# Keys of a chunk in parts of 512 and 384 instead of 448 and 448, and a new order of the first blocks' loads and query products

## The reference, cut to what matters

```python
q = (query @ Wq + bq).reshape(B, L, NKV, G, HDIM)          # 64 x 4096, 8 groups of 4 heads
k_, v_ = jnp.split(kv @ Wkv + bkv, 2, axis=-1)             # 6272 x 1024 each
scores = jnp.einsum('blkgd,bmkd->bkglm', q, k) * scale
attn = jax.nn.softmax(scores, axis=-1)
o = jnp.einsum('bkglm,bmkd->blkgd', attn, v).reshape(B, L, NHEAD * HDIM)
return o @ Wo + bo
```

## Time and profile before

| what | value |
|---|---|
| median of 3 runs | 1019.71 us |
| lowest and highest | 1017.62 and 3386.0 us |
| the profiled execution's own time | 1017.49 us |
| its span, first to last instruction | 1015.7 us |
| mean granted TensorE clock | 0.998 |
| PE busy | 996.8 us (98%) |
| DVE busy | 744.5 us (73%) |
| ACT busy | 587.4 us (58%) |
| POOL busy | 441.6 us (43%) |

### The profile page before, as it was taken

How to read it: one execution, slowest core, us unless ns; L and a number is a source line. 1 busy time by engine, 2 the same in 40 slices (tenths; PEclk the granted TensorE clock), 3 DMA queues, 4 the chain that set the end, 5 groups by cost and what they waited for, 6 DMA issues and landing times.

```text
span 1015.7 us, 20355 instructions
## 1 busy us (share of the span) xinstructions
PE 996.8 (98%) x7083; PEld 922.3 (91%) x7083; DVE 744.5 (73%) x1680; ACT 587.4 (58%) x1254; POOL 441.6 (43%) x641
## 2 busy tenths in 40 slices
PE   8989999999999999999999999999999999999998
PEld 6769999999999999999999999999999999999744
DVE  5677877676877777777877778677777768776666
ACT  5455666565656656566665656565665655565431
POOL 2243544444434545344454445434444444333231
PEclk9999999999999999999999999999999999999999
DMA  9763332333424333333333333333333237464895
GB/s 323 229 218 128 107 129 98 133 120 131 138 93 134 106 129 112 113 131 130 129 107 115 107 133 122 125 118 117 128 107 133 93 125 245 161 220 157 254 329 162
DMA packets 90085, 149.59 MB, mean 147 GB/s; under 512 B 10528, under 2 KB 44976, under 8 KB 89984
## 3 DMA queue, kind: packets, MB, share of 16 engines
q1 hardware_dynamic: 88224, 146.42, 43.6%
q10 hardware_dynamic: 1424, 1.51, 0.4%
q0 software_dynamic: 336, 0.35, 0.1%
HBM read 82.97 MB, written 14.81 MB: 96 GB/s over the span
## 4 chain that ended last, share of the span: by engine, by line
PE 91%; DVE 4%; DMA 2%; ACT 1%; issue 1%; SPq 1%; POOL 0%; DVEq 0%; POOLq 0%; ACTq 0%
PE p_kv L88 16%; PE p_kv L90 16%; PE p_kv L89 15%; PE p_s L88 7%; PE p_s L90 6%; PE p_s L89 6%; PE p_t L769 6%; PE p_o L88 4%; PE p_o L90 4%; PE p_o L89 4%; PE p_s L849 1%; PE p_ot L753 1%; DMA wkv_raw<-in_wkv 1%; DMA ctx_st<-in_ctx_t 1%; PE p_o L783 1%
## 5 line engine op out<-in xcount | busy, mean ns | idle before, releaser
L610 POOL TENSOR_SCALAR slots<-code 128x512 f32<-128x512 bf16 x232 | 147.8, 637 | 247.3 <-DVE slots L1466 164.2
L1210 ACT ACTIVATE pt_hi<-p_t 128x512 fp32r<-128x512 f32 x224 | 110.0, 543 | 117.0 <-PE p_t L769 111.4
L1466 DVE TENSOR_TENSOR slots<-slots 128x512 f32<-128x512 f32 x232 | 169.8, 732 | 1.6 <-POOL slots L610 1.5
L1239 ACT ACTIVATE slots<-code,drop_and_offsets 128x512 f32<-128x512 bf16 x232 | 158.6, 713 | 6.5 <-POOL code L606 3.4
L1198 ACT ACTIVATE v_hi<-p_kv 128x256 fp32r<-128x256 f32 x196 | 75.3, 384 | 139.1 <-PE p_kv L90 138.3
L630 POOL TENSOR_TENSOR slots<-slots 128x512 f32<-128x512 f32 x58 | 77.7, 1339 | 165.5 <-DVE slots L1466 165.5
L1430 DVE TENSOR_TENSOR pt_lo<-p_t,pt_hi 128x512 fp32r<-128x512 f32 x224 | 128.7, 614 | 11.0 <-ACT pt_hi L1210 10.0
L1415 DVE TENSOR_TENSOR v_lo<-p_kv,v_hi 128x256 fp32r<-128x256 f32 x196 | 83.1, 424 | 67.4 <-ACT v_hi L1198 64.7
L88 PE MATMUL p_kv<-wkv_hi,ctx_even_hi 128*128 128x256 f32 x448 | 128.9, 288 | 0.2 <-DVE v_lo L1415 0.2
L89 PE MATMUL p_kv<-wkv_lo,ctx_even_hi 128*128 128x256 f32 x448 | 125.9, 281 | 0.0
L90 PE MATMUL p_kv<-wkv_hi,ctx_even_lo 128*128 128x256 f32 x448 | 125.9, 281 | 0.0
(11 more groups left out here) (261 smaller groups left out, 2717.5 us busy)
## 6 DMA issues: line engine op xcount, KB each, us to landing
probs_r<-probs SPq DMA_DIRECT2D x110, 448.0 KB, 3.7
code<-in_codes SPq DMA_DIRECT2D x58, 256.0 KB, 3.8
scale<-in_scales SPq DMA_DIRECT2D x114, 128.0 KB, 3.1
expanded_weights<-slots SPq DMA_DIRECT2D x56, 256.0 KB, 2.1
ctx_st<-in_ctx_t SPq DMA_DIRECT2D x96, 112.0 KB, 3.0
ring_hi<-expanded_weights SPq DMA_DIRECT2D x22, 256.0 KB, 5.4
ring_lo<-expanded_weights SPq DMA_DIRECT2D x22, 256.0 KB, 5.6
wq_hi<-in_wq SPq DMA_DIRECT2D x4, 1024.0 KB, 7.2
```

The costliest lines, as they stand in the source:

```text
L610: nc.gpsimd.tensor_scalar(slots[:, slot, :], code16[:], LINES[j][0], LINES[j][1], ALU.mult, ALU.add).then_inc(pool_lines, 1)
L1210: nc.scalar.activation(pt_hi[:, at:at + n, :].rearrange("p t q -> p (t q)"), p_t[:, c % 2, 0:n * ROWS], ACT.Copy).then_inc(pt_rounded, 1)
L1239: nc.scalar.activation(slots[:, slot, :], code16[:], ACT.Identity, bias=offsets[:, k:k + 1], scale=LINES[j][0]).then_inc(act_lines, 1)
L1466: nc.vector.tensor_tensor(slots[:, slot, :], slots[:, slot, :], slots[:, other, :], ALU.max).then_inc(merged, 1)
```

## The change

The two halves of 448 keys become parts of 512 and 384 keys: wherever a key product, a score, a rounding, a split or a score statistic took `HALF` columns, it now takes `part_keys(c)`. The number of instructions stays, and so does the sum of their columns. In the first part of chunk 0 the pieces of the next chunk's context are moved to later places. In block 2, query product 7 on PE goes behind the first four value products, and the turn of query 7 into the value tiles; on DVE `finish_query(6)` and `finish_query(7)` move forward. In the last block `project_out(0)` moves behind two value and transpose steps.

```diff
-HALF = CHUNK // 2
+EDGES = (0, 4 * P, CHUNK)
+def part_keys(c, n=1):
+    return slice(EDGES[c], EDGES[c + n])
+def part_width(c):
+    return EDGES[c + 1] - EDGES[c]
...
-    elif pair < 2:
-        piece = ((0, 1, PIECES, 2, 3), (4, PIECES, 5, 6, 7))[pair][place]
+    elif pair == 0:
+        piece = (0, 1, PIECES, PIECES, 2)[place]
...
         def k_place(h, c):
-            return p_s[:, 0, 0:HALF] if c == 0 else p_kv[:, h % 2, 0:HALF]
+            return p_s[:, 0, 0:part_width(0)] if c == 0 else p_kv[:, h % 2, 0:part_width(1)]
...
-                keys = slice(c * HALF, (c + 1) * HALF)
+                keys = part_keys(c)
...
                         m = split_matmuls(nc, s_place(h, c, r), q_hi[:, h, r * P:(r + 1) * P],
-                                          q_lo[:, h, r * P:(r + 1) * P], k_hi[:, c * HALF:(c + 1) * HALF],
-                                          k_lo[:, c * HALF:(c + 1) * HALF])
+                                          q_lo[:, h, r * P:(r + 1) * P], k_hi[:, part_keys(c)],
+                                          k_lo[:, part_keys(c)])
...
# TensorE, block_work
                 next_keys(i, h, half, 0)
+                weigh_values(i - 1, 0, SPLIT_TILE)
                 if i == 2:
                     query_product(7)
-                weigh_values(i - 1, 0, SPLIT_TILE)
                 turn_probs(i - 1, 2)
...
                 for t in value_tiles(i)[:SPLIT_TILE]:
+                    if i == 2 and t == 2:
+                        query_turn(7)
                     value_tile(i, h, half, t)
-                if i == 2:
-                    query_turn(7)
                 next_keys(i, h, half, 1)
...
# TensorE, last_block
-                project_out(0)
                 weigh_values(i - 1, 0, SPLIT_TILE)
                 turn_probs(i - 1, 2)
                 turn_probs(i - 1, 3)
+                project_out(0)
                 project_out(1)
...
# VectorE, block_work
                 split_probs(i - 1, 1)
+                if i == 2:
+                    finish_query(6)
                 merge(i, 0)
...
                 merge(i, 2)
-                if i == 2:
-                    finish_query(6)
...
                     split_wkv(h + 2)
+                if i == 2:
+                    finish_query(7)
                 for t in tiles[3:]:
                     split_values(i, t)
                 split_keys(i, h, 1)
                 if i == 2:
-                    finish_query(7)
                     add_output(0, 0)
```

More of the change, by code:

```diff
@@ L240, in k_place @@
         def k_place(h, c):
-            return p_s[:, 0, 0:HALF] if c == 0 else p_kv[:, h % 2, 0:HALF]
+            return p_s[:, 0, 0:part_width(0)] if c == 0 else p_kv[:, h % 2, 0:part_width(1)]
         def s_place(h, c, r):
-            return p_s[:, r, 0:HALF] if c == 0 else p_kv[:, r if h % 2 == 0 else 1 - r, 0:HALF]
+            if c == 0:
+                return p_s[:, r, 0:part_width(0)]
+            return p_kv[:, r if h % 2 == 0 else 1 - r, 0:part_width(1)]
         RING_ODD = 6
@@ L1201, in round_keys @@
                 nh = (h + 1) % NKV
-                round_kv(kv_number["k", i, c], k_hi[:, c * HALF:(c + 1) * HALF], k_place(h, c), bk_sb[:, nh:nh + 1])
+                round_kv(kv_number["k", i, c], k_hi[:, part_keys(c)], k_place(h, c), bk_sb[:, nh:nh + 1])
             def round_values(i, t):
@@ L1266, in round_first @@
                 act.wait_ge(first_in[k], 16)
-                keys = slice(c * HALF, (c + n) * HALF)
+                keys = part_keys(c, n)
                 nc.scalar.activation(even_hi[:, k, keys], ctx_raw[:, k, keys], ACT.Copy).then_inc(first_rounded, 1)
@@ L1420, in split_keys @@
             def split_keys(i, h, c):
-                nh, keys = (h + 1) % NKV, slice(c * HALF, (c + 1) * HALF)
+                nh, keys = (h + 1) % NKV, part_keys(c)
                 split_kv(kv_number["k", i, c], k_lo[:, keys], k_place(h, c), k_hi[:, keys], bk_sb[:, nh:nh + 1])
@@ L1453, in score_stats @@
                         dve.wait_ge(scores_psum, 4 * i + 2 * c + r + 1)
-                        nc.vector.tensor_scalar(probs[:, r, c * HALF:(c + 1) * HALF], s_place(h, c, r), -SCALE, None,
+                        nc.vector.tensor_scalar(probs[:, r, part_keys(c)], s_place(h, c, r), -SCALE, None,
                                                 ALU.mult, ALU.min,
```

## The result

| | kernel before | changed kernel |
|---|---|---|
| median, 6 runs each | 1020.62 us | 1012.56 us (1011.21 to 1012.73) |
| ratio to before | | 0.9931, 95% interval 0.9913 to 0.9950 |
| the profiled execution's own time | 1017.49 us | 1012.23 us |
| span | 1015.7 us | 1010.4 us |

One of the six executions of the kernel before took 3386.0 us; it is in its median and not in the ratio. The change gains 7.0 us (5.1 to 8.9). The forecast was 1012.0 us within 1003 to 1019.

A forecast was written before the change was run, and what follows sets the result against it. PE was taken as the bound (busy 98% of the span, 91% of the chain). Gains of 6.3 us in blocks 1 and 2 and 0.4 in the last gave 1010.8 us like the profiled execution, median 1012, range 1003 to 1019.

The forecast's parts named there:

- The sizes, taken at 0: All blocks: a pair of 512 and 384 columns costs what two of 448 cost, 406.4 ns in the middle; 0 us.
- Rivals 1 and 3: Matmul cost: 1, mostly 13.3 ns beside columns, 1005.5 us, chance 0.13; 3, wide matmul pays another step, 1025 us, 0.05.
- The cover of part 1: Each block: smaller part 1 and longer first scores (0.16 us) give its key chain more cover; counted as nothing.
- The new wait of 1.2 us: Block 2: PE's value products wait for probabilities held up on ACT by context piece 2, landing at 65.3 us; 1.2 us lost.
- Rival 2: Piece 2 takes 10.1 us to land, PE waits 4.5 us, the clock falls (1.5 us): 1016.8 us, chance 0.12.
- Holes 1 to 3: PE's waits in blocks 1 and 2 before: 2.26 us for k_lo, 2.54 for query 6, 0.87 for query 7; all to go.
- the net of 6.3 us: Blocks 1 and 2: 7.5 us gained from waits and clock, less the new 1.2 us wait.
- The queries, 2.7 + 0.9 us: Block 2: earlier finish_query(6) and finish_query(7) on DVE remove PE's waits for these queries, 2.7 and 0.9 us.
- No hole, no fall: Behind the k_lo wait the clock read 0.50; without that wait it should not fall, gaining 1.5 us.
- The last block, 0.4 us: Value products placed ahead of project_out(0) start earlier, when DVE's splits end; 0.4 us gained, bounds 0 and 1.3 us.
- The median: Changed kernel's median forecast at 1012 us, from 1010.8 us for an execution like the profiled one; chance 0.57.

The follow-up runs named there:

- PE only: Kernel before with query product 7 behind the first value products and query 7's turn between value tiles, DVE's order unchanged: 1016.83 us, ratio 0.9978.
- whole order with old sizes and early weights: Changed kernel with parts of 448 and the weight loads of queries 6 and 7 issued ahead of the first expanded tile's store: 1010.18 us, ratio 0.9905.
- early weights alone: Kernel before with only the weight loads of queries 6 and 7 issued ahead of the first expanded tile's store: 1014.51 us, ratio 0.9951.

## Why the prediction was right, step by step

- **The sizes, taken at 0: right.** Blocks 3 to 54 took 850.23 to 850.39 us in the four profiles with 512 and 384 columns, and 849.71 to 850.66 in the ten with 448. Rivals 1 and 3 fall with that. The cover of part 1 was enough: no block waits for `k_lo`.
- **The new wait of 1.2 us: right in size, by two errors.** Piece 2 landed at 58.56 + 8.4 = 67.0 us, not at 65.3, and the splits ended at 70.70, not at 69.1. PE too came 1.8 us later than forecast (69.7, not 67.9); 1.4 of them it had lost ahead of block 2. It waited about 1.1 us. Rival 2 was thus half true: the piece was late, its mark (an ACT wait past 67 us) was just reached, and the clock did not fall. The prediction held against it that "a load lands once what was issued ahead of it has". That reading was wrong. The two weight slabs (60.0 and 63.6), the codes (66.7) and the piece (67.0) did land in the order of their issue, but the first of the two moves of probabilities, issued 4 us behind the second slab, landed 6.4 us later at 62.7, ahead of that slab. SP's issues:

```profile
52.24 0.63 SPq L498 DMA_DIRECT2D wq_lo<-in_wq  x1
56.35 1.15 SPq L485 DMA_DIRECT2D probs_r<-probs  x2
```

  The trace of the kernel before shows it too: the move issued at 55.98 landed at 61.8, ahead of the slab issued at 51.63 (62.1) and the piece issued at 52.31 (62.4). The rule of the Trainium skill that was cited for rival 2 (DMA: Bandwidth & Descriptors, "Queues, rings and completion order"), that completion need not be first in, first out, agrees with both.
- **What was left out:** 1.43 us ahead of block 2. 0.31 of it is there at block 0's scores (18.62 to 19.02 us in the four profiles with the new sizes, 18.18 to 18.75 in the ten with the old ones; the ranges overlap, so it is not shown that the sizes cost it). The other 1.1 us come at the wait for query 6's weights. They were issued 0.6 us later than before (51.60, 50.99), and their load took 8.4 us instead of 7.6; this differs from one execution to the next, 7.0 us in the changed kernel's second one, so a part of the 1.1 us is that execution's chance. I had asked what a moved piece does to ACT, and taken the rest of SP's queue as it was. So block 3 came 4.7 us earlier, not 6.3.
- **Holes 1 to 3, the clock and the net of 6.3 us: near in block 2 alone (6.11 measured), 1.3 us too high for blocks 1 and 2 together (5.0 measured, from 41.2 to 36.2 us), and the split was wrong.** The step that failed is "That is 2.61 us less one matmul: 2.4 us. In the new order no context piece stands there." It credited 2.4 + 1.5 us to the pieces' place. Alone, that place gave 0.6 us (-0.4 to 1.7). ACT's stand was only moved, the expansion behind the backlog stayed late, and finish_query(6) stood behind it on DVE: hole 2 took what hole 1 gave. And "What is late next?" was asked of the keys, not of the query.
- **The queries, 2.7 + 0.9 us: the mechanism was right, the size too small.** Alone they gave 6.4 us (4.9 to 7.9). The term that was put in the wrong place is the clock: "No hole, no fall" booked the fall on hole 1 alone, at 1.5 us. A fall between 60 and 80 us stands in all five profiles in which DVE finishes query 6 late and the weights come late (before twice, sizes, pieces, PE only), behind hole 1, hole 2 or both, and in none of the nine others; hole 1 stood for 2.93 us with the queries moved on DVE only, without a fall. Its price is the clock that is missing. In the kernel before that is 0.07, 0.50 and 0.28 of three stretches of 2 us, the middle one in the earlier trace rows, so 1.7 us in all:

```profile
64.00:66.00 2.00, 0.67 (x3) 0.61 (x4) 1.40 (x4) 1.10 (x4) 1.74 (x3) 0.93 0.46 137
...
68.00:70.00 2.00, 2.00 (x14) 1.93 (x13) 1.43 (x6) 1.43 (x4) 0.28 (x1) 0.72 1.04 370
```

  With the pieces alone it is 3.4 us (72 to 80), twice as much; that and the longer hole 2 used up what hole 1 gave in that execution. The time of block 2 bears this out. It took 19.42 us in the whole order with old sizes and early weights, which has no hole. Of the 7.65 us more before, 5.67 are the three waits of the earlier trace rows and 2.0 are left; with the pieces alone 9.63 less 6.3 of waits leaves 3.3. So early weights alone (5.0 us) and the queries alone (6.4) can't be added: with the last block they give 9.0 together, as the fall, which is absent with either edit, counts once. The clocks of all timed executions agree: the mean over an execution was 0.995 to 0.998 in all 66 of the kernel before in the experiments, and 0.998 to 1.000 in all 40 of the kernels that have the new order on DVE or the early weights. At which place the clock was missing, such a mean doesn't tell.
- **The last block, 0.4 us: right** (0.5 us). From block 55's first score to the end it took 76.60 to 76.63 us in the eight profiles with the old order of the last block and 76.10 to 76.14 in the six with the new one. The new order still waits, now for DVE's splits, as the earlier trace rows let expect:

```profile
939.28 0.36 PE L100 MATMUL p_o<-pt_hi,v_hi 128*128 128x256 f32 x1 [1.00 <-issue]
```

- **The median: right, with help.** The profiled execution came out at 1012.23 us, 1.4 above the sum, for the reasons above; the changed kernel's median lies only 0.3 us above it, where 1.2 had been allowed. The two differences nearly cancel: that the median came within 0.6 us of the forecast is luck.

What stays open: what decides whether the clock falls behind a hole, and why the load of query 6's weights took 8.4 us in one execution of the changed kernel and 7.0 in the other, and PE waited 1.60 and 0.22 us for it.

## What to carry to other kernels

Several waits within a few microseconds can be one backlog met by several engines: before pricing them one by one, ask what was issued late on the queue, and whether the DMA engines ran empty just ahead of it (two loads sent ahead of a store that wasn't ready gave 2.3 us here). Moving the instruction that waits only handed the wait on here; taking the urgent step out from behind a slow side job on an engine that works in order (DVE's finishing of a query behind the expansion) gave 6.3 us, the end of a fall of the clock included. A right sum does not show that its terms are right: kernels with one edit each do.

## What the hardware showed that was not expected

**The granted clock behind the same hole is not always the same.** In every profile PE waits 1.36 or 1.37 us for the first query's low part just before block 0's scores. In five of fourteen profiles the clock then read 0.50 to 0.55 from 20 to 22 us, as in the changed kernel's second execution, where the first had 1.00 (the stretch from 20 to 24 us, the second execution first):

```profile
20.00:24.00 4.00, 4.00 (x17) 2.91 (x18) 2.95 (x11) 2.56 (x4) 1.84 (x3) 0.57 1.02 355
```

```profile
20.00:24.00 4.00, 3.47 (x27) 2.32 (x25) 2.38 (x10) 3.23 (x7) 1.54 (x3) 1.00 1.03 370
```

From block 0's to block 1's first score it took 30.7 us with the fall (49.36 - 18.63 in the whole order with old sizes) and 29.2 us without (47.90 - 18.69), and within 0.1 us of these in the other twelve profiles: 1.5 us that one execution has and another has not, as much as several terms of the sum. Nor does the length of a hole alone settle it between 60 and 80 us: falls stand behind 2.26, 3.00, 3.04, 3.14, 3.66 and 4.90 us, none behind 1.30, 2.28, 2.54, 2.88 and 2.93. The Trainium skill (TensorE: Matmul & The Clock Gate, "What's actually happening") holds that the half rate is the default and activity lifts it; the runs agree in that every fall follows a stand of PE, and add that the same stand brings it or not.

**A matmul's distance grew in proportion to its columns.** The prediction read two levels, 13.3 and 19.7 ns beside the columns. Rows of the changed kernel (scores of one block: five distances of 512 columns between the first two rows, five of 384 between the last two):

```profile
474.61 0.39 PE L100 MATMUL p_s<-k_hi,q_hi 128*128 128x512 f32 x1
...
475.77 0.40 PE L102 MATMUL p_s<-k_hi,q_lo 128*128 128x512 f32 x1
476.01 0.34 PE L100 MATMUL p_kv<-k_hi,q_hi 128*128 128x384 f32 x1
...
476.88 0.34 PE L102 MATMUL p_kv<-k_hi,q_lo 128*128 128x384 f32 x1
```

That is 1.16 / 5 = 232 ns and 0.87 / 5 = 174 ns, 18.7 and 14.0 ns beside the columns at 2.4 GHz. Both are 0.453 ns a column, as are 448 columns at 203 ns, the mean of the two distances in the earlier trace rows. A pair costs 406 ns, inside the prediction's 400.0 to 412.8. A cost that follows the columns leaves any split of a chunk alone, and that is what the times show.
